# Cross attention's scores: 64-row products in two row tiles, against full-height products with stacked queries

## What is computed

```
q = (layernorm(x) @ Wq.T + bq)   heads of 32        k = (ctx @ Wk.T + bk)   heads of 32
scores = q . k / sqrt(32);  attn = softmax(scores);  out = attn . v
x = x + out @ Wo.T + bo
```

## Time and profile before

| | |
|---|---|
| median of 3 runs | 3448.6 us (3447.24 to 3449.78) |
| span of the profiled execution | 3449.3 us |
| PE busy | 3303.4 us (96%) |
| DVE busy | 2186.2 us (63%) |
| ACT busy | 1775.7 us (51%) |
| POOL busy | 1132.9 us (33%) |
| cross phase, about | from 42 us to 570 us of the span |

### The profile page before, as it was taken

The page is one execution under the profiler, slowest core; times in us unless marked ns, Lnnn a source line. Parts: engine busy times, 40 slices in busy tenths (PEclk is TensorE's granted clock), DMA queues, the critical chain, the costliest instruction groups (busy, mean ns, idle before and its releaser), DMA issues. The chain is left out here.

```text
span 3449.3 us, 51260 instructions
## 1 busy us (share of the span) xinstructions
PE 3303.4 (96%) x17680; PEld 2696.6 (78%) x17680; DVE 2186.2 (63%) x4999; ACT 1775.7 (51%) x4490; POOL 1132.9 (33%) x1011
## 2 busy tenths in 40 slices
PE   6999998999999989999999989999999899999999
PEld 5666676788888868888888868888888688888887
DVE  6887876899999984222332259998999643333332
ACT  5666664788878863111111248887888521121111
POOL 3443443655555520000000045555555111111011
PEclk9999999999999999999999999999999999999999
DMA  4112204122111232111111121111121321111110
GB/s 127 44 47 67 73 32 141 38 71 65 62 62 62 62 94 93 34 45 44 44 45 45 67 67 62 62 62 62 64 71 61 123 93 51 51 45 39 51 39 34
DMA packets 186899, 215.92 MB, mean 63 GB/s; under 512 B 27142, under 2 KB 125702, under 8 KB 186643
## 3 DMA queue, kind: packets, MB, share of 16 engines
q1 hardware_dynamic: 186643, 212.65, 19.1%
HBM read 125.79 MB, written 69.00 MB: 56 GB/s over the span
## 5 line engine op out<-in xcount | busy, mean ns | idle before, releaser
L2124 DVE SCALAR_TENSOR_TENSOR u_full<-banks,b_cols,gate 128x512 f32<-128x512 f32 (+1 forms) x176 | 132.0, 750 | 855.3 <-ACT gate L2083 855.3
L2083 ACT ACTIVATE gate<-banks,b_cols 128x512 f32<-128x512 f32 (+1 forms) x176 | 121.3, 689 | 995.6 <-PE banks L48 995.6
L46 PE MATMUL banks<-fxT_h,w_h 128*128 128x512 f32 (+1 forms) x1408 | 550.0, 391 | 2.4 <-DVE w_l L2109 2.3
L47 PE MATMUL banks<-fxT_l,w_h 128*128 128x512 f32 (+1 forms) x1408 | 549.5, 390 | 0.0
L48 PE MATMUL banks<-fxT_h,w_l 128*128 128x512 f32 (+1 forms) x1408 | 549.4, 390 | 0.0
L1979 POOL TENSOR_TENSOR sums<-sums,b_rows 128x512 f32<-128x512 f32 x64 | 84.9, 1358 | 844.7 <-DMA sums<-z_rows 844.7
L1322 PE MATMUL banks<-pT,v 128*128 128x256 f32 x1440 | 355.5, 368 | 4.2 <-DVE oT_l L1638 4.2
L1340 PE MATMUL banks<-ident,prob 128*128 128x128 f32 x1440 | 341.5, 277 | 14.3 <-DVE neg_m L1595 13.1
L1199 POOL TENSOR_TENSOR rn<-ssq,neg_half 128x8 f32<-128x8 f32 x128 | 210.9, 1647 | 399.0 <-DVE ssq L1566 392.8
L46 PE MATMUL banks<-wqkv_h,hT_h 128*128 128x512 f32 x768 | 322.7, 420 | 7.4 <-DVE hT_l L1558 7.1
L46 PEld LDWEIGHTS banks<-fxT_h,w_h 128*128 128x128 f32 (+1 forms) x1408 | 260.5, 185 | 64.2 <-DVE w_l L2109 4.0
(11 more groups left out here) (190 smaller groups left out, 7628.1 us busy)
## 6 DMA issues: line engine op xcount, KB each, us to landing
y_rows<-sums SPq DMA_DIRECT2D x16, 1024.0 KB
sums<-y_rows SPq DMA_DIRECT2D x64, 256.0 KB, 2.9
z_rows<-sums SPq DMA_DIRECT2D x64, 256.0 KB, 2.0
sums<-z_rows SPq DMA_DIRECT2D x16, 1024.0 KB, 5.8
thirds<-in_w SPq DMA_DIRECT2D x30, 512.0 KB, 4.9
thirds<-in_x SPq DMA_DIRECT2D x8, 1024.0 KB, 6.6
thirds<-y_rows SPq DMA_DIRECT2D x64, 128.0 KB, 2.7
thirds<-y_late SPq DMA_DIRECT2D x64, 128.0 KB, 3.2
```

Of the source, the lines that this page charges most:

```text
L46: pe.matmul(out, a_h, b_h, start=start, stop=False)
L47: pe.matmul(out, a_h, b_l, start=False, stop=False)
L2124: e.scalar_tensor_tensor(out=u_full[r, m % 2, :], in0=ps[r, 2 * (m % 2), :], scalar=b1[r, place[m], 0:1], in1=gate[r, :], op0=ALU.add, op1 ...
```

## The change

The queries' two tiles `qT` (value, rest) become one tile `q_hl` with a place for each pair. For pair 0 the value lies in partitions 0 to 63 and the rest in 64 to 127; for pair 1 the other way round. `k_bd` gets twice the size: for each pair the two heads' keys stand in rows 0 to 63 and once more in rows 64 to 127. A score tile is then, for each pair, one product of all 128 rows with the rounded keys and one with the rests of the keys: 4 matmuls of 128 rows and 308 columns in place of 6 of 64 rows. (The product of both rests is computed too.) `hi_q` and `lo_q` become two instructions of 64 partitions each; `lo_q` writes to the half that it does not read. `keys_in_place` makes 8 copies on each of its engines in place of 4, and `load_keys` issues 16 DMAs for each half in place of 8. Semaphore counts go with it.

```diff
+HEAD_ROWS = 2 * XD
-                    k_bd=sb("k_bd", [P, DC, 2, SC]),
+                    k_bd=sb("k_bd", [P, DC, 2, 2, SC]),
-                    xT=sb("xT", [P, DC, G]), qT=sb("xqT", [P, DC, G]), bq=sb1("bq_cols", [P, DC]),
+                    xT=sb("xT", [P, DC, G]), q_hl=shared.enter_context(nc.sbuf_tensor("q_hl", [P, DC, 2, G], F32R)), bq=sb1("bq_cols", [P, DC]),
+def key_rows(r):
+    return [slice(HEAD_ROWS * copy + r % 2 * XD, HEAD_ROWS * copy + r % 2 * XD + XD) for copy in range(2)]
+def query_rows(pair, rest):
+    copy = pair ^ rest
+    return slice(HEAD_ROWS * copy, HEAD_ROWS * copy + HEAD_ROWS)
...
 def load_keys(e, keep, dram, b, half):
...
         for r in range(QUAD):
-            e.dma_start(keep["k_bd"][part][r * XD:(r + 1) * XD, c, r % 2, :].bitcast(F32),
-                        src[r * XD:(r + 1) * XD, c]).then_inc(keep["ld_k"][half], 16)
+            for rows in key_rows(r):
+                e.dma_start(keep["k_bd"][part][rows, c, r // 2, r % 2, :].bitcast(F32),
+                            src[r * XD:(r + 1) * XD, c]).then_inc(keep["ld_k"][half], 16)
...
             for r in range(QUAD):
-                dst = keep["k_bd"][part][r * XD:(r + 1) * XD, :, r % 2, :]
                 src = kT[part][r * XD:(r + 1) * XD, :, 0:SC].bitcast(F32)
-                if part:
-                    e.tensor_copy(dst, src).then_inc(bd_k, 1)
-                else:
-                    e.activation(dst, src, ACT.Copy).then_inc(bd_k, 1)
+                for rows in key_rows(r):
+                    dst = keep["k_bd"][part][rows, :, r // 2, r % 2, :]
+                    if part:
+                        e.tensor_copy(dst, src).then_inc(bd_k, 1)
+                    else:
+                        e.activation(dst, src, ACT.Copy).then_inc(bd_k, 1)
...
                     for pair in range(2):
-                        r = slice(64 * pair, 64 * pair + 64)
-                        last = split_matmul(e, ps[:, 2 * (n % 2) + pair, 0:2 * SC],
-                                            [x[r, c % DC, tt * P:(tt + 1) * P] for x in qT],
-                                            [x[r, c % DC, :, :].rearrange("p a s -> p (a s)") for x in k_bd], True, True)
+                        for part in range(2):
+                            last = e.matmul(ps[:, 2 * (n % 2) + pair, 0:2 * SC], q_hl[:, c % DC, pair, tt * P:(tt + 1) * P],
+                                            k_bd[part][:, c % DC, pair].rearrange("p a s -> p (a s)"), start=part == 0, stop=part == 1)
...
                 def hi_q(it, c):
                     e.wait_ge(pe_q, DC * it + (c + 1))
-                    e.activation(qT[0][:, c % DC, :], ps[:, TURNS, :], ACT.Identity, bias=bq[:, c % DC:c % DC + 1]).then_inc(ac_q, 1)
+                    for pair in range(2):
+                        r = query_rows(pair, 0)
+                        ins = e.activation(q_hl[r, c % DC, pair, :], ps[r, TURNS, :], ACT.Identity, bias=bq[r, c % DC:c % DC + 1])
+                    ins.then_inc(ac_q, 1)
...
                 def lo_q(it, c):
                     e.wait_ge(ac_q, DC * it + (c + 1))
-                    e.scalar_tensor_tensor(out=qT[1][:, c % DC, :], in0=ps[:, TURNS, :], scalar=bq[:, c % DC:c % DC + 1],
-                                           in1=qT[0][:, c % DC, :].bitcast(F32), op0=ALU.add, op1=ALU.subtract).then_inc(dv_q, 1)
+                    for pair in range(2):
+                        r = query_rows(pair, 0)
+                        ins = e.scalar_tensor_tensor(out=q_hl[query_rows(pair, 1), c % DC, pair, :], in0=ps[r, TURNS, :],
+                                                     scalar=bq[r, c % DC:c % DC + 1], in1=q_hl[r, c % DC, pair, :].bitcast(F32),
+                                                     op0=ALU.add, op1=ALU.subtract)
+                    ins.then_inc(dv_q, 1)
```

More of the change, by code:

```diff
@@ L248, in context_phase @@
         v = [x[0:SCH] for x in wk]
-        x_in, xn, stats, mv, ve, rs, xT, qT, bq = (keep[n] for n in ("x_in", "first_xn", "stats", "mv", "ve", "rs", "xT", "qT", "bq"))
+        x_in, xn, stats, mv, ve, rs, xT, q_hl, bq = (keep[n] for n in ("x_in", "first_xn", "stats", "mv", "ve", "rs", "xT", "q_hl", "bq"))
         wq = keep["wq"]
@@ L387, in _ @@
                 e.wait_ge(keep["pe_q"], 1)
-                e.activation(qT[0][:, 0, :], ps[:, TURNS, :], ACT.Identity, bias=bq[:, 0:1]).then_inc(keep["ac_q"], 1)
+                for pair in range(2):
+                    r = query_rows(pair, 0)
+                    ins = e.activation(q_hl[r, 0, pair, :], ps[r, TURNS, :], ACT.Identity, bias=bq[r, 0:1])
+                ins.then_inc(keep["ac_q"], 1)
             @block.vector
@@ L432, in _ @@
                 e.wait_ge(keep["ac_q"], 1)
-                e.scalar_tensor_tensor(out=qT[1][:, 0, :], in0=ps[:, TURNS, :], scalar=bq[:, 0:1],
-                                       in1=qT[0][:, 0, :].bitcast(F32), op0=ALU.add, op1=ALU.subtract).then_inc(keep["dv_q"], 1)
+                for pair in range(2):
+                    r = query_rows(pair, 0)
+                    ins = e.scalar_tensor_tensor(out=q_hl[query_rows(pair, 1), 0, pair, :], in0=ps[r, TURNS, :], scalar=bq[r, 0:1],
+                                                 in1=q_hl[r, 0, pair, :].bitcast(F32), op0=ALU.add, op1=ALU.subtract)
+                ins.then_inc(keep["dv_q"], 1)
 def cross_phase(nc, io, ps, ident, sem, neg_half, dram, keep, y, ahead):
@@ L451, in cross_phase @@
     rows_of = [min(P, QW - k * P) for k in range(QK)]
-    K_LOADED, V_LOADED = 16 * 2 * QUAD, 16 * 2 * len(SEGMENTS)
+    K_LOADED, V_LOADED = 16 * 2 * 2 * QUAD, 16 * 2 * len(SEGMENTS)
     LEAD = 1 + GT
@@ L472, in sb @@
             return st.enter_context(nc.sbuf_tensor(name, shape, dt))
-        xT, qT, bq, stats, mv, ve, rs = (keep[n] for n in ("xT", "qT", "bq", "stats", "mv", "ve", "rs"))
+        xT, q_hl, bq, stats, mv, ve, rs = (keep[n] for n in ("xT", "q_hl", "bq", "stats", "mv", "ve", "rs"))
         bo = sb("bo_rows", [P, D])
```

## The result

The changed kernel takes 3501.9 us (median; 3500.2 to 3504.6) against 3448.4 us for the kernel before on the same chip. The ratio is 1.0151, 95% interval 1.0139 to 1.0163: 53.6 us slower. The forecast was 3489 us, 40 us slower, so the direction and most of the size came as worked out, and 13 us were missing. The profiled execution of the changed kernel has a span of 3498.1 us, 48.8 more than the profiled one before.

A forecast was written before the change was run, and what follows sets the result against it. The prediction took PE's waits behind the queries' split to set the cross phase, no engine being full. Split 40.1, scores −2.8 and context +2.9 gave +40.2 us on 3448.6, so 3489 us, range 3463 to 3503.

The forecast's parts named there:

- What bounds the phase: Cross phase: no engine is full; three of four places of the queries' split hold a gap or wait behind it.
- The scores on PE: Cross phase's score tiles: a lone tile saves 0.15 us, a group 0.35, 8 groups 2.8 us.
- The split: Queries' halves on ACT and DVE at four places: each costs a whole, +5.3 us a group, 40.1 us in all.
- (1,3): Place of the queries' split where PE waits for a rest of the probabilities behind lo_q: +1.6 us, 8 times.
- (3,3): Place of the queries' split where scores start just behind lo_q: +1.6 us for the transposes after them, 7 times.
- (0,2): Place of the queries' split where PE waits for lo_q itself to get its bank back: +1.35 us, 8 times.
- the other bound: Queries' split with full overlap of instructions: 1.23 us for both engines, 29.8 us in all, forecast 3478.5 us.
- The context phase and the reload: ACT's four more key copies add 2.9 us before the first scores; the reload's 8 more DMAs a half cost nothing.
- PE sets the pace and hides the split: Rival, outside the full stretch: split hidden, 3443.5 us, or 3440.6 if the context's part is hidden too; 12% with both.
- a part is soaked up: Rival, queries' split: delays at neighbouring places overlap or halves are cheap, so +20 us, 3469 us; 13%.
- the turns don't go away: Rival, scores on PE: each product pays a slot and a start, +0.3 us a group, 3494 us; 5%.
- The late reload: Rival: value loads late, or DVE halves also hold back what comes before: +5 to +12, 3494 to 3501 us; 10%.

The follow-up runs named there:

- split_only: The kernel before with only hi_q and lo_q each written as two instructions of 64 partitions, old scores and keys: 3500.5 us, ratio 1.0149.
- queries_twice: The kernel before with hi_q and lo_q each preceded by a whole copy into a spare tile, all starting at partition 0: 3491.4 us, ratio 1.0119.
- whole_queries: The changed kernel with hi_q and lo_q each one whole instruction, so its scores multiply other numbers: 3447.1 us, ratio 0.9993.
- filled_both: The changed kernel with unread matmuls in PE's waits, 11 for that at (1,3) and 8 at (0,2): 3492.7 us, ratio 1.0122.
- changed_split_last: The changed kernel with, at (1,3), hi_q behind hi_p and hi_x, lo_q behind lo_p and lo_x: 3481.2 us, ratio 1.0096.
- before_split_last: The kernel before with, at (1,3), hi_q behind hi_p and hi_x, lo_q behind lo_p and lo_x: 3445.3 us, ratio 0.9994.

## Why the prediction was right, and what it lacked

**What bounds the phase.** Right. PE's 92% in the cross phase said little; the gaps behind `hi_q` and `lo_q` said where the change would cost. `split_only` shows it: the loss comes with 31 instructions more on each of two engines, which idle a third and a fifth of the phase.

**The scores on PE.** Right in mechanism, and slightly too small. The pairs of 64 rows run together, the turn in and out costs what two slots do, and without it a lone tile saves 0.14 us (0.15 forecast). A group gains 0.60 us with whole queries where I gave 0.35, because all three tiles in the stretch of projections count in full (0.45) and some behind it add 0.15. Over 8 groups it is 2 us more than forecast; beside the halves, whose waits and clock take part of it back, a group shows less (71.47 against 71.65 us).

**The split.** Right. At the places themselves, from the start of `hi_q` to what PE does behind it: (1,3) 3.91 − 2.21 = +1.70 (forecast 1.6); (3,3) and (0,2), from

```profile
189.23 1.37 ACT L800 ACTIVATE q_hl<-banks,bq_cols 64x512 fp32r<-64x512 f32 x2
...
192.21 0.42 PE L684 MATMUL banks<-k_bd_h,q_hl 128*128 128x308 f32 x1 [1.49 <-DVE q_hl L886]
...
201.21 1.40 ACT L800 ACTIVATE q_hl<-banks,bq_cols 64x512 fp32r<-64x512 f32 x2
...
204.31 0.47 PE L47 MATMUL banks<-xwo_h,xoT_h 128*128 128x512 f32 x1 [2.30 <-DVE q_hl L886]
```

2.98 against 1.55 and 3.10 against 1.85, so +1.43 for the scores (1.5) and +1.25 (1.35). As a sum for a group, the full-clock group with halves less that with whole queries, it is 69.70 − 64.27 = 5.43 us where 5.3 had been forecast. Choosing the row of the key copies, that instructions on changing partitions don't overlap, was the right choice between the bounds; `queries_twice` shows the other bound as worked out. That choice rested on ACT alone, and held on DVE: its two halves take 1.51 us, two whole ones start 0.67 apart. The Trainium skill ("VectorE: DVE Perf Modes", Two Vector instructions with no wait between them) states the hold for DVE. The traces agree with it.

**The context phase and the reload.** As far as can be told, right: +2.9 forecast, 2.4 measured with the keys alone (−0.3 to +5.9 by the interval), nothing for the reload. The kernel after has its first scores at 46.78 and not 45.3, but `whole_queries`, which does the same work up to there, has them at 44.66, so 2 us of that is spread from one execution to the next.

**The clock.** This is the step that failed. The prediction read the clock of the group before the change, 1.00, and took every duration behind the places at that clock. It named PE's brackets of 2.7 and 2.1 us to come (3.15 and 2.30 came) and did not ask what a PE that idles so long is granted afterwards. The clock stood in its sum at nothing. The price shows between the changed kernel and `filled_both`: 71.47 − 69.70 = 1.8 us a group. From (0,2) of group 0 to (0,2) of group 7 the trace after takes 488.7 us against 442.8, +45.9. `filled_both` takes 477.8 for the same stretch, so 35.0 were foreseen in kind (7 × 4.95 = 34.7 forecast) and 10.9 go with the clock. With the 3 us ahead of it that makes the 48.8 us between the two spans; the medians differ by 5 us more. The changed kernel's profiled execution, at 3500.25 us, accounts for 1.7 of them, being that much below its median; what makes up the rest stays open.

**The rivals.** That PE sets the pace and hides the split is refuted by `split_only`. That a part is soaked up was not the case: no stretch came out at half. That the turns don't go away is refuted by the 0.80 us. The late reload did not happen. The loss of clock was in none of them. That 3501.9 us still lies inside the stated range, whose high end was 3503, is luck: the rival that gave 3494 to 3501 us had a late reload or a longer hold on DVE for its reason, and neither came.

## What to carry to other kernels

Cost a change by the waits that stand behind it in order on its engine: the halves on two engines that had time to spare took 0.8 to 1.7 us of the phase at each of their four places, while the saving on the busiest engine was worth 0.6 us a group. Splitting an instruction by partitions saves nothing on ACT and DVE, and it loses the overlap with its neighbours. When a change lengthens PE's idle times, price the matmuls behind them at half the clock as a case of its own: behind a wait of 3.15 us the fall came in every full group of the changed kernel and cost 1.2 to 1.8 us, behind one of 2.3 us it came in every group, in four of six or in none, depending on the kernel. And before giving up a change that adds work to an in-order queue, look whether the work can stand behind what PE needs first (here some 20 of 54 us).

## What the runs showed that I had not expected

- The granted clock fell from 1.00 to 0.50 behind an idle time of PE of 3.15 us in a phase with PE 86% busy, and 19 unread matmuls a group that kept PE busy there made the kernel 9 us faster. It depends on more than one wait: with the longest one filled, the clock fell in four of six groups behind another of 2.3 us, in `changed_split_last` it never fell behind one of 2.33 us, and in `before_split_last` it fell in two groups at one of 1.18 us that every group has.
- A fall of the clock need not cost anything. In group 4 of the changed kernel it fell behind (3,3) too (a mean of 0.86 from there to (0,2)), and the stretch still took 11.98 us: PE's wait for `lo_q` at (0,2) shrank from 2.30 to 1.53 us.
- Two matmuls on 64 rows each, of different pairs, start together and cost one slot, but a lone score tile of six costs 0.71 us for 0.42 us of slots. Four on all rows take 0.57 us with nothing around them.
